# Spreading the routing weights of the experts in pairs of products on separate halves of the array rows, with one bank for the side products

## The reference, cut to what matters

```python
shared = silu(xf @ Ws_up) @ Ws_down
aff = xf @ centroids.T
_, idx = top_k(aff + expert_biases, 8)
w = sigmoid(take_along_axis(aff, idx, axis=1))
w = w / (sum(w, axis=-1, keepdims=True) + 1e-08)
cw = zeros((T, E)).at[arange(T)[:, None], idx].add(w)
h = silu(einsum('td,edf->etf', xf, W_up))
y = einsum('etf,efd->etd', h, W_down)
return shared + einsum('etd,te->td', y, cw)
```

## Time and profile before

| | |
|---|---|
| median of 3 runs | 1983.4 us (1980.77 to 1983.73) |
| span of the profiled execution | 1978.2 us |
| what lies around it, against the median | 5.2 us |
| TensorE busy, whole span | 1579.2 us (80%), mean granted clock 0.883 |
| VectorE, ScalarE, GpSimd busy | 1410.5, 1163.7, 998.2 us |
| spread products (L1701) | 256, median 379 ns |
| up and down products | 264 each on lines 1670, 1671, 1672 for `ub`, as many for `e_yb` |
| experts stage | about 1509 us to the end |

### The profile page before, as it was taken

How to read it: one execution, slowest core, us unless ns; L and a number is a source line. 1 busy time by engine, 2 the same in 40 slices (tenths; PEclk the granted TensorE clock), 3 DMA queues, 4 the chain that set the end, 5 groups by cost and what they waited for, 6 DMA issues and landing times. The chain is left out here.

```text
span 1978.2 us, 32338 instructions
## 1 busy us (share of the span) xinstructions
PE 1579.2 (80%) x9101; PEld 752.0 (38%) x9101; DVE 1410.5 (71%) x2630; ACT 1163.7 (59%) x1991; POOL 998.2 (50%) x923
## 2 busy tenths in 40 slices
PE   3599989898988889945764677777664999999998
PEld 2245444444444445422442122222222444444443
DVE  5677868686868687827766988898998555555554
ACT  1177766666667677625544444443333777777776
POOL 4144535353535353425862455544441667777776
PEclk7699989998999999976887777777777999999999
DMA  4332212131313131000003000000000000000000
GB/s 104 92 100 58 85 50 85 46 89 39 96 36 99 36 99 41 22 1 0 1 0 86 0 1 0 0 0 0 0 0 0 1 6 6 5 5 5 0 6 11
DMA packets 51217, 64.95 MB, mean 33 GB/s; under 512 B 7980, under 2 KB 42440, under 8 KB 51080
## 3 DMA queue, kind: packets, MB, share of 16 engines
q1 hardware_dynamic: 49640, 61.12, 10.8%
q10 hardware_dynamic: 1440, 2.10, 0.3%
HBM read 34.36 MB, written 28.05 MB: 32 GB/s over the span
## 5 line engine op out<-in xcount | busy, mean ns | idle before, releaser
L804 DVE TENSOR_REDUCE bmax<-p1b 128x4 f32<-128x512 f32 x640 | 408.5, 681 | 117.4 <-PE p1b L621 110.6
L553 ACT ACTIVATE pT<-p2b 128x512 f32<-128x512 f32 x640 | 373.2, 595 | 173.5 <-PE p2b L636 172.2
L1618 POOL TENSOR_TENSOR hid_l<-e_hid,hid_h 128x512 f16<-128x512 f32 x264 | 305.4, 1160 | 139.3 <-ACT hid_h L1758 138.2
L619 PE MATMUL p1b<-ks,qs 96*128 96x512 bf16 (+3 forms) x1024 | 274.0, 314 | 59.4 <-DVE bmax L804 33.0
L1864 DVE TENSOR_TENSOR e_hid<-act_u,e_cb 128x512 f32<-128x512 f32 x256 | 174.8, 687 | 187.6 <-ACT act_u L1772 163.5
L530 POOL TENSOR_SCALAR_AFFINE_SELECT pT<-pT 128x1280 f32<-128x1280 f32 (+2 forms) x192 | 162.3, 876 | 241.5 <-ACT pT L553 241.5
L636 PE MATMUL p2b<-qs,ks 96*128 96x512 bf16 (+3 forms) x1024 | 253.5, 310 | 7.3 <-ACT pT L553 6.7
L1772 ACT ACTIVATE act_u<-ub 128x512 f32<-128x512 f32 x264 | 157.3, 596 | 83.6 <-PE ub L1672 82.4
L621 PE MATMUL p1b<-causal,identb 128*128 128x128 bf16 x1024 | 200.1, 227 | 0.0
L649 PE MATMUL ob<-pT,vs 128*32 128x512 f32 (+3 forms) x2048 | 196.1, 456 | 2.2 <-POOL pT L530 2.2
L1479 DVE TENSOR_TENSOR_SCAN hs<-dA,dBx 128x512 f32<-128x512 f32 x128 | 183.3, 1432 | 17.0 <-ACT dA L1385 11.0
(11 more groups left out here) (254 smaller groups left out, 3027.5 us busy)
## 6 DMA issues: line engine op xcount, KB each, us to landing
qs<-q_stacks SPq DMA_DIRECT2D x64, 204.0 KB
q_stacks<-parts SPq DMA_DIRECT2D x96, 128.0 KB
k_stacks<-parts SPq DMA_DIRECT2D x96, 128.0 KB
ks<-k_stacks SPq DMA_DIRECT2D x64, 192.0 KB
qs<-nparts SPq DMA_DIRECT2D x192, 4.0 KB
out_dram<-x_tok SPq DMA_DIRECT2D x8, 256.0 KB, 2.3
wmod<-L_wmod SPq DMA_DIRECT2D x2, 384.0 KB, 5.8
q_stacks<-zeros SPq DMA_DIRECT2D x4, 192.0 KB, 3.1
```

The lines of the kernel that those rows point to most:

```text
L553: act.activation(pT[:, g2 % 2, v, :], p2b[v % 2][:, :], ACT.Exp, scale=SCALE).then_inc(exp_done, 1)
L619: pe.matmul(bank[:, at * P:(at + c + 1) * P], qs[:, slot, m, c * P:(c + 1) * P], ks[:, slot, m, 0:(c + 1) * P], start=True, stop=False, sk ...
L804: dve.tensor_reduce(to, src, AX, ALU.max).then_inc(first_read, 1)
L1618: pool.tensor_tensor(hid_l[:, place(T), :], hid[:, place(T), :], hid_h[:, place(T), :], ALU.subtract).then_inc(split_ready, 1)
```

## The change

The 64 experts are split into two halves: slot T (even) now takes the pair T/2 of the first 32 experts, slot T + 1 the pair T/2 of the last 32 (`experts_of`). `parts` is laid out so that rows 0 to 63 hold the high and the low part for the first 32 experts, rows 64 to 127 those for the last 32. The two spread products of the slots T and T + 1 have 64 rows each, on the two halves of the array's rows, and are issued one behind the other in the even slot, into two of now four banks `e_cb`. The banks for this come from the side products, which now all use one bank, `e_sideb`. For this their steps are moved: everything for the next batch from `pre_turn` on comes six slots later (top 8 and the rest too, the split of `parts` seven), except GpSimd's `e_hTl`, which stays in slot 10; and waits are added (`pre_turn` for the residual, `turn_back` for `parts`). VectorE copies the weights in two halves and scales the two low parts singly. The hardware loop now has three turns of two rounds each.

```diff
-        pick = sb("e_pick", [P, ET, 2], FP16)
-        sel = sb("sel_e", [P, ET, P], FP16)
+        pick = sb("e_pick", [P, PAIRS, 2], FP16)
+        sel = sb("sel_e", [P, PAIRS, P], FP16)
-        cw = sb("cw", [P, TILES, 2, E])
+        cw = sb("cw", [P, TILES, 2, 2, HALF_E])
-        cb = [ps(f"e_cb{i}") for i in range(2)]
-        yb, preb, routeb, postb = ps("e_yb"), ps("e_preb"), ps("routeb"), ps("e_postb")
+        cb = [ps(f"e_cb{i}") for i in range(4)]
+        yb, sideb = ps("e_yb"), ps("e_sideb")
+        def experts_of(T):
+            return T // 2 + PAIRS * (T % 2) if T < ET else ET
+        def share_bank(T):
+            return T % 4
+        def bank_or_last(T):
+            return share_bank(T) if T < ET else None
...
-            with eng.Fori(1, B - 1) as r:
-                step(r, pre=True, main=True, post=True)
+            with eng.Fori(0, B // 2 - 1) as it:
+                step(it * 2 + 1, 1, pre=True, main=True, post=True)
+                step(it * 2 + 2, 0, pre=True, main=True, post=True)
...
                 def pre_turn():
                     pe.wait_ge(xn_ready, b + 1)
                     pe.wait_ge(low_read, b + 1)
+                    if post:
+                        pe.wait_ge(x_ready, r + 1)
...
+                def spread(T):
+                    pe.wait_ge(hid_ready, free(r * SLOTS + T, T, bank_or_last))
+                    pe.wait_ge(hid_ready, free(r * SLOTS + T + 1, T + 1, bank_or_last))
+                    for j in range(2):
+                        rows = slice(2 * HALF_E * j, 2 * HALF_E * (j + 1))
+                        pe.matmul(cb[share_bank(T + j)][:, :], sel[rows, T // 2, :], parts[rows, a, :], start=True, stop=True).then_inc(c_done, 1)
...
-                        if T < ET:
-                            pe.wait_ge(hid_ready, free(q, T, bank))
-                            pe.matmul(cb[bank(T)][:, :], sel[:, T, :], parts[:, r % 2, :], start=True, stop=True).then_inc(c_done, 1)
+                        if T < ET and T % 2 == 0:
+                            spread(T)
                         if pre:
-                            for at, f in ((3, pre_turn), (7, route), (20, turn_weights)):
+                            for at, f in ((9, pre_turn), (13, route), (26, turn_weights)):
...
-                            for at, f in ((4, pre_h), (10, sigmoid), (21, high)):
+                            for at, f in ((10, pre_h), (16, sigmoid), (27, high)):
...
-                    dve.tensor_copy(cw[:, :, :, :], rest[:, :, :].unsqueeze(2).broadcast_to([P, TILES, 2, E])).then_inc(cw_ready, 1)
+                    for j in range(2):
+                        ins = dve.tensor_copy(cw[:, :, j, :, :], rest[:, :, j * HALF_E:(j + 1) * HALF_E].unsqueeze(2).broadcast_to([P, TILES, 2, HALF_E]))
+                    ins.then_inc(cw_ready, 1)
...
-                    dve.tensor_tensor(low[E:2 * E, :], preb[E:2 * E, :], lo, ALU.subtract).then_inc(low_read, 1)
+                    dve.tensor_tensor(low[:, :], sideb[:, :], parts[:, 1 - a, :], ALU.subtract).then_inc(low_read, 1)
                     dve.wait_ge(low_read, b + 2)
-                    dve.tensor_scalar(lo, low[E:2 * E, :], LOW, None, ALU.mult).then_inc(parts_ready, 1)
+                    for at in (HALF_E, 3 * HALF_E):
+                        rows = slice(at, at + HALF_E)
+                        ins = dve.tensor_scalar(parts[rows, 1 - a, :], low[rows, :], LOW, None, ALU.mult)
+                    ins.then_inc(parts_ready, 1)
```

More of the change, by code:

```diff
@@ L6 @@
+import itertools
 import math
@@ L1513, in experts @@
     SLOTS = ET + 1
+    PAIRS = ET // 2
+    HALF_E = E // 2
     RING = 5
@@ L1601, in _, with step @@
             pool.wait_ge(consts, 1)
[L1602 to L1609, removed]
+            for n, (j, s, a) in enumerate(itertools.product(range(2), range(2), range(2))):
+                view = pick[:, :, a]
+                pool.affine_select(out=view, in_=view, compare_op=ALU.not_equal, fill=W_SCALE / LOW if s else W_SCALE,
+                                   base=-2 * HALF_E * j - HALF_E * s - a, pattern=[[-2, PAIRS]], channel_multiplier=1).then_inc(consts, 1)
+                pool.wait_ge(consts, 2 + n)
+            def step(r, a, pre, main, post):
                 def split_h():
@@ L1639, in _, with step @@
             pe.wait_ge(k.w_ready, W_CHUNKS)
-            pe.transpose(preb[:, 0:E], cent[:, :], k.ident[0:E, 0:E]).then_inc(cent_psum, 1)
+            pe.transpose(sideb[:, 0:E], cent[:, :], k.ident[0:E, 0:E]).then_inc(cent_psum, 1)
             pe.wait_ge(cent_ready, 1)
-            def step(r, pre, main, post):
+            def step(r, a, pre, main, post):
                 b = r + 1
@@ L1697, in step @@
                         pe.wait_ge(silu_ready, free(q, T, bank))
-                        product(ub[bank(T)][:, :], weights(0, T), hTh[:, r % 2, :], hTl[:, r % 2, :], True, True).then_inc(u_done, 1)
-                        if T < ET:
-                            pe.wait_ge(hid_ready, free(q, T, bank))
-                            pe.matmul(cb[bank(T)][:, :], sel[:, T, :], parts[:, r % 2, :], start=True, stop=True).then_inc(c_done, 1)
+                        product(ub[bank(T)][:, :], weights(0, T), hTh[:, a, :], hTl[:, a, :], True, True).then_inc(u_done, 1)
+                        if T < ET and T % 2 == 0:
+                            spread(T)
                         if pre:
-                            for at, f in ((3, pre_turn), (7, route), (20, turn_weights)):
+                            for at, f in ((9, pre_turn), (13, route), (26, turn_weights)):
                                 if T == at:
@@ L1751, in high @@
                     act.wait_ge(parts_ready, b + 2)
-                    act.activation(parts[:, b % 2, :], preb[:, :], ACT.Copy).then_inc(high_ready, 1)
+                    act.activation(parts[:, 1 - a, :], sideb[:, :], ACT.Copy).then_inc(high_ready, 1)
                 def round_hidden(r, T):
@@ L1869, in step @@
                         if pre:
-                            for at, f in (*steps, (21, split)):
+                            for at, f in (*steps, (28, split)):
                                 if T == at:
```

45 lines of the change are left out of this document (23 added, 22 removed).

## The result

| | before | after |
|---|---|---|
| median of 5 runs on one chip | 1980.77 us (1976.09 to 1983.73) | 1989.45 us (1987.39 to 1991.02) |
| ratio | | 1.0045, 95% interval 1.003 to 1.006 |
| profiled execution, span | 1978.2 us | 1987.4 us |
| last stage, from its first product to the end | 468.88 us | 477.87 us |
| its rounds 1 to 6, first product to first product | 55.65, 55.39, 55.40, 55.39, 55.40, 55.35 | 56.93, 54.70, 59.82, 54.69, 59.88, 54.78 |

The kernel became slower, by 0.45%. The last stage is longer by 9.0 us, which is the whole difference of the spans. From here on stages are compared, since the last stage begins up to 7 us earlier or later from one execution to the next. Each stage time is that of one profiled execution, and it is called shown by the runs too only where the ratio of the medians says so.

What follows compares the result with a forecast made beforehand. TensorE sets the pace, but a chain through VectorE and GpSimd sets slot 3. Terms -0.3 + 2.6 + 1.3 + 0.3 + 0.5 - 0.4 = +4.0 us on 1978.2, plus 5.2 to the runs' median: 1987 us, range 1963 to 2000.

Steps and rivals of the forecast that it cites:

- the pairs: Spread products on TensorE: side by side but with changes of tile, 0.43 us against 0.432; -0.3 us over 128.
- the transposes: Next batch's four fp32 transposes, moved from slot 3 to slot 9: 0.44 us each round, +2.6 us in six rounds.
- the prologue's half a microsecond: VectorE's split weight copy and scaling before the rounds delay the first up product: +0.5 us once.
- rival (2): The two halves do not run side by side; each pair costs 0.65 us, total 2010 us; chance 0.12.
- Rival (1): Change of tile costs little, or only on one side, and halves run together: 1965 or 1975 us; chance 0.21.
- The stall (a): TensorE's slot 3 wait, traced to VectorE's four normalizations held by GpSimd: +0.2 us a round, +1.3 us in six.
- rival (4): The slot 3 stall shrinks since the normalizations get in ahead of GpSimd: 1982 us; chance 0.05.
- VectorE's halves: Weight copy and low-part scaling as two instructions each: 0 in the rounds, up to +1.16 us a round, +8 us.
- rival (3): VectorE's second halves wait for GpSimd in each round: +8 + 4, 1995 us; chance 0.07.
- The loop: Three branches back go, shortening TensorE's idle 0.17 us at a round's start: -0.1 us each, -0.4 us.
- (b): TensorE's slot 13 wait for ScalarE's table loads round the sigmoid: stays as long within 0.05 us; +0.3 in the sum.

Runs made afterwards that it cites:

- run with whole rows: The changed kernel with each pair's two products over all 128 rows, zeros for the other half, so no change of tile; 1982.87 us, ratio 1.002.
- run on the same half: The changed kernel with both products of a pair on rows 0 to 63, so they cannot run side by side; one run, 2009.71 us.
- The loop alone: The kernel before with only its six middle rounds made three turns of two on all engines; 1986.29 us against 1979.45, ratio 1.003.

## Why the prediction was right or wrong

The forecast was +4 us, and +8.7 us was measured between the medians (9.0 in the stage). That the pairs would be no gain was right. That the kernel would be slower came true mostly for other reasons than mine: of the 9 us only the 2.6 of the transposes and the prologue's half a microsecond are the ones that I had summed. With three more activations ahead of the loop the same change comes out at 1.0007, the "same" to which I had given 0.29; so the direction was partly luck. By the sign that I had named (a round below 55 us or above 57) its mechanism is wrong: there are rounds of 54.7 and of 59.8 us.

- **The pairs, 0.43 against 0.432 us: right.** The parts are as worked out: a change of tile of some 0.095 us each way, 0.01 us behind it. The run with whole rows shows the equality, the one on the same half that rival (2) is false: had they run one behind the other, the stage would be some 20 us longer. Rival (1), a cheap change of tile, is false as well. The Trainium skill, "TensorEngine Tiling (Array Packing)", Key Properties, says that a change of the tiling mode drains the engine; the trace agrees, with 0.095 us more at each of the two changes. The speedup of its section Theoretical Speedup, up to twofold, is there for the pair by itself (the run on the same half takes 0.22 us more), and paid back in full here, since a pair of 512 columns is all that stands between two changes.
- **The transposes, +2.6 us: right.** 0.44 us each time, in six rounds.
- **The stall (a), +1.3 us: wrong.** "The third normalization would then get in ahead of GpSimd, but not the fourth" was a race of a tenth of a microsecond that I settled once for all rounds. The +0.2 us can be seen in no round. Round 1 kept its length (7.98 us in slots 0 to 3, 8.01 before), and the third normalization waited there. In the even rounds all four got in, the lower bound of my own range, and gave 1.0 us back each time. The very order that I had forecast stands in the even rounds of the run with ScalarE's loop back at one round, and there the slots take 7.70 us, 0.06 less than before and not 0.2 more: GpSimd's operation came 0.2 us later, as I said, but the wait of the third normalization was gone. The order follows how late ScalarE's first silu is: GpSimd's next operation starts 1.50 us behind the first normalization in round 2, where the silu is 0.93 us behind the round's start, 1.40 us where it is 1.03 behind, and 1.17 us in round 1 (1591.11 and 1589.94), where it is 1.23 behind. (For rival (4), my own terms give 1981 us and not 1982: +4 without the 1.3, less 5.)
- **VectorE's halves, 0: wrong, +2.6 us in three rounds.** This is rival (3), which I had at 1.16 us in every round. It came in the odd ones, at 1.0 us: there the second half asks 0.1 us behind GpSimd's start (1754.05 against 1753.94). In the run on the same half it came in no round, so this too is a matter of the order.
- **The loop, -0.4 us: the step that failed most, +6.3 us.** I took it for "three of the branches back go" and looked only at the branches. Nothing in the trace of before showed the cost of a longer body, since one round's body never stalled, and I had put no upper bound on it. The loop alone, and the three activations, show it: +3.1 and +3.2 us at the two jumps back, where ScalarE stands still and code is read again. A saving of 0.13 us a round is real (slot 32 lasts 1.50 us against 1.63), but it isn't the branches: it is there also in rounds 2 and 4, which end in a jump back. Its cause is open.
- **(b), +0.3 us: 0.** The two slots of the sigmoid take 2.6 and 2.4 us in both kernels.
- **The statement "a round should take 55.9 to 56.1 us"** held for none. A round would have had no length of its own to state once the body had two of them.

By the summed slots: +6.3 (code) - 3.0 (a) + 2.6 (transposes) + 2.35 (halves, less the 0.13 us in rounds 2 and 4) + 0.8 (start) = +9.0, rounded. Of these the code's part is shown by the loop alone and the three activations, by their runs too; the halves' by one run's timeline, the transposes' by the timeline alone. That the normalizations' order makes up the even rounds' gain is shown by the run with one of them a slot, in the other kernel, and by the run in which ScalarE's loop changed and the gain went with the order. What stays open is why the order falls as it does in each round of a kernel; it turns on less than 0.1 us, and the three activations alone changed it in rounds 1 and 6. How much of the +0.8 at the start is the prologue's second scaling is measured (0.43 us, by the run without it); the rest isn't.

## What to carry to other kernels

Price a new loop body as an edit of its own: a body of several rounds may no longer stay in the engine's instruction memory, and then each jump back costs microseconds, not the branch's time; look for "issue" at an engine's first operation behind a jump, or for a named releaser that had long been done (VectorE above), and for packets of the instruction queue beside it. Packing products in halves of the array pays only where several stand between two changes of tile. And where a cheap VectorE operation waits for GpSimd's, spread a bunch of them out rather than hope for the order: the bunch is what the next engine waits for, and 0.1 us decides which way it falls.

## What the runs showed of the hardware that I had not expected

- ScalarE stood 3.7 to 3.8 us at a jump back, beside five packets of 8 KB in the instruction queue, and three small instructions ahead of the loop took that away. VectorE still started 1.6 us late there, beside two packets.
- In round 5 TensorE idled 1.71 us, ran three products and a pair, idled 0.61 us, and then ran six products at half the clock: they start 0.43 us apart, not 0.22, and the granted clock (the third value from the end of the first row, by stretch) was 0.50, the lower level, 1.2 GHz. In round 3, with idle times of 1.65 and 0.61 us at the same places, it stayed at 1.00:

```profile
1820.10:1822.10 2.00, 2.00 (x5) 0.69 (x6) 2.00 (x4) 0.21 (x1) 1.01 (x1) 0.50 0.00 0
```
```profile
1820.46 0.63 PE L1686 MATMUL e_yb<-hid_l,w_high 128*128 128x512 f16 x1
1820.89 0.63 PE L1687 MATMUL e_yb<-hid_h,w_low 128*128 128x512 f16 x1
```

- Two row halves that both write all 128 partitions of PSUM, in two banks, start 3 ns apart and disturb each other by nothing that the starts show.
- GpSimd's difference itself takes 1.30 us, not 1.16, where VectorE's normalizations were in ahead of it (1762.55 above): the wait goes both ways.
